# A transformer layer with AdaLN, window attention and an expert FFN: the input stage joined to attention

## The chip, the core and the metric

The kernel runs on one core of a Trainium2 chip. The core has five engines that run their own instruction streams and meet at semaphores: TensorE (PE; PEld is its weight load) multiplies, VectorE (DVE) and ScalarE (ACT) do elementwise work and reductions, GpSimd (POOL) does elementwise work more slowly and issues indirect transfers, and SyncE (SP) issues the other transfers, which 16 DMA engines carry out. The metric is the device time of one execution in microseconds (us).

## What is computed

The input has 2 batches of 2048 tokens with 256 values each. Per batch, six modulation rows come from a small vector c; two of them (ga, gb) are gates.

```
mod = (silu(c) @ wmod).reshape(B, 6, 1, -1)          # c: 2x256, wmod: 256x1536
sa, ca, ga, sb, cb, gb = the six rows of mod
ga, gb = (2 * (g >= 0) - 1) * maximum(abs(g), 0.25)  # each of them
h = layernorm(x) * (1 + ca) + sa
x = x + ga * attention(h, Wqkv, Wout)                # 16 heads of 64, causal window of 128
h = layernorm(x) * (1 + cb) + sb
x = x + gb * moe_ffn(h)                              # 8 experts, the 2 best for each token, capacity 640
```

## The kernel before

The 4096 tokens are 8 chunks of 512 (NC = 8), a chunk is 4 tiles of 128 (TILES), and 8 pairs of heads (PAIRS) stand for the 16 heads. All products with the weights are done with a value split in two fp16 parts, a high one and a low one, and three matmuls for each (SPLIT_PRODUCTS). So every weight is split before its first use: the high part is the scaled weight in fp16, the low part the scaled weight less the high part.

There are three blocks, each with one program for each engine, and a barrier of all engines between them. The first is the input stage, the second attention with routing, the third the FFN.

**Input stage.** SyncE issues, in this order: c (cT), all of the modulation weights (wmod, 1.5 MB, in the memory of k), the gate weights (gwT, gbB), the first chunk of x, Wqkv in three parts of 1 MB and Wout (stage 0 to 3; the first two lie where q will be, the others where attn will be), the other 28 tiles of x in one, and b1T. GpSimd makes the constants, then the rstd of chunk 0, then the low parts of stage 2 and 3. ScalarE waits for all the small loads, makes exp(-c), and then the high parts; stage 2 and 3 take it two passes. VectorE makes silu(c) and a copy of it spread over 128 columns (silB), the statistics and normalised rows xn of chunk 0, the modulation columns (modcol: ca and sa, with the features on the partitions), the low parts of stage 0 and 1, and the modulation rows. TensorE multiplies modcol's products and, with silB as weights, the rows' products on all 128 partitions, one batch after the other (score[0] and score[1]). VectorE makes modrow of them (the row of sb, 1 + cb and the two gates), again on all partitions and batch by batch.

**Attention's head.** VectorE clears the halos of k and v. TensorE transposes chunk 0's xn; ScalarE applies modcol to it (h32, ln_modulate); VectorE casts the high part (ln_high) and GpSimd subtracts the low part (ln_low). Then TensorE projects chunk 0 in pairs, q0, k0, q1, k1 and so on (HEAD_QK), through two PSUM banks (gen), which ScalarE empties. Then come the transposes of chunk 1's rows and LAG = 4 steps in which the scores of the first heads and the v projection of chunk 0 alternate. VectorE merges the scores, finds the maximum and normalises; ScalarE does the exponentials. For chunk 2 VectorE makes the statistics (ln_first(2)) and the normalised rows (ln_second(2)). From there chunk after chunk runs in one pattern: `scores`, `weighted_values`, `transposes`, and the projections of the next chunk between them.

**SyncE in attention.** It first fills slot_inputs in DRAM with empty rows (80 transfers), waits for them, and then stores the chunks. GpSimd waits for the same fill at the end of chunk 0, before the rstd for chunk 3. GpSimd's pieces in a chunk are the two masked copies for each unit (split_keys), the low part of the next rows, and, from chunk 1 on, the routing's scatter.

## Time and profile before

| | us |
|---|---|
| median of 3 runs | 1242.08 (1242.06 to 1242.58) |
| profiled execution | 1242.26 |
| its span, first to last instruction | 1240.5 |
| TensorE busy | 1131.4 (91%) |
| VectorE busy | 785.8 (63%) |
| ScalarE busy | 680.3 (55%) |
| GpSimd busy | 505.6 (41%) |

The busy shares are means over stages of different kinds. A window is a stretch of the span, with the busy time of each engine in it. In a row of the timeline the first number is the start and the second the length, both in us from the span's start, and a bracket at the end gives how long the engine had been idle before and what released it. A row can stand for several instructions (xN). L numbers are lines of the kernel before. "SPq" rows are issues of transfers: their length is the time that the issue took SyncE, and not that of the transfer.

### The profile page before, as it was taken

How to read it: one execution, taken by the hardware profiler on the slowest of the kernel's cores; microseconds unless marked ns; L12 is line 12 of the kernel's file. 1: busy time of each engine (PE TensorE's matmuls, PEld its weight loads, DVE VectorE, ACT ScalarE, POOL GpSimd, SP SyncE). 2: the span in 40 equal slices, each digit the busy share in tenths (PEclk: the TensorE clock that was granted, in tenths of full speed). 3: DMA queues.
4: the chain of work that ended last, by engine and by line, in shares of the span. 5: the costliest groups of instructions: out<-in, count | busy, mean ns of one | idle time of the engine just before them, and what ended most of it. 6: DMA issues, size and time to landing. Idle time of an engine off the chain costs nothing. (4 is left out here: it accounts for less than half of the span.)

```text
span 1240.5 us, 26348 instructions
## 1 busy us (share of the span) xinstructions
PE 1131.4 (91%) x10008; PEld 749.8 (60%) x10008; DVE 785.8 (63%) x1713; ACT 680.3 (55%) x1882; POOL 505.6 (41%) x558
## 2 busy tenths in 40 slices
PE   3799999999999999999999771499999999999996
PEld 2355565655655655656556551276868677686865
DVE  6366577486576575675865833476767667666754
ACT  4377657476477476475774721365472746547261
POOL 2134244454465255444544642414242434424242
PEclk9799999999999999999999975699999999999998
DMA  9641000100100001000002100613232233432000
GB/s 299 155 162 53 2 18 2 36 18 15 40 2 31 23 2 35 19 1 30 19 10 63 45 26 27 214 37 117 88 95 103 82 119 98 143 108 81 21 18 9
DMA packets 64858, 76.45 MB, mean 62 GB/s; under 512 B 18144, under 2 KB 56164, under 8 KB 64608
## 3 DMA queue, kind: packets, MB, share of 16 engines
q1 hardware_dynamic: 53984, 53.25, 13.5%
q0 software_dynamic: 10752, 21.54, 5.3%
q8 instruction: 80, 1.31, 0.5%
q14 instruction: 42, 0.34, 0.1%
HBM read 48.93 MB, written 33.78 MB: 67 GB/s over the span
## 5 line engine op out<-in xcount | busy, mean ns | idle before, releaser
L1230 ACT ACTIVATE hid<-up,b1T 128x512 f16<-128x512 f32 (+1 forms) x192 | 123.3, 642 | 196.1 <-PE up L1164 171.4
L1179 PE MATMUL down<-w,hid 128*128 128x256 f16 x1920 | 214.5, 273 | 0.0
L1164 PE MATMUL up<-xT,w 128*128 128x512 f16 (+1 forms) x1152 | 210.5, 344 | 0.0
L976 POOL TENSOR_SCALAR_AFFINE_SELECT probT_split<-probT 128x512 f32<-128x512 f32 x128 | 99.3, 776 | 261.7 <-ACT probT L688 261.1
L1179 PEld LDWEIGHTS down<-w,hid 128*128 128x128 f16 x1920 | 187.3, 98 | 23.1
L469 PE MATMUL gen<-hT,big 128*128 128x512 f16 x768 | 186.4, 382 | 10.9 <-ACT h2T L705 4.0
L680 ACT ACTIVATE prob<-score,negmax 128x128 f32<-128x128 f32 x512 | 180.4, 373 | 2.9 <-DVE negmax L797 2.9
L1120 POOL DMA_INDIRECT out<-y,rows x80 | 79.8, 998 | 238.3 <-DVE y L1296 226.0
L1164 PEld LDWEIGHTS up<-xT,w 128*128 128x128 f16 x1152 | 112.4, 98 | 93.3 <-issue 0.5
L1267 DVE TENSOR_TENSOR hid<-hid 128x512 f16<-128x512 f32 (+1 forms) x192 | 115.4, 607 | 77.1 <-ACT hid L1232 58.9
L792 DVE COPY_PREDICATED score<-above,score 128x512 f32<-128x512 int32 x128 | 88.4, 691 | 92.2 <-PE score L503 91.9
L688 ACT ACTIVATE probT<-pt 128x512 f32<-128x512 f32 x128 | 76.6, 598 | 106.2 <-PE pt L519 105.2
L1232 ACT ACTIVATE hid<-up,b1T 128x512 f32<-128x512 f32 (+1 forms) x192 | 123.6, 644 | 0.0
L469 PEld LDWEIGHTS gen<-hT,big 128*128 128x128 f16 x768 | 73.5, 98 | 80.6 <-ACT h2T L705 5.0
L503 PE MATMUL score<-k,q 64*64 64x192 f32 x2048 | 115.0, 339 | 0.2 <-ACT prob L680 0.2
L680 ACT ACTIVATION_READ_ACCUMULATOR prob<-score,negmax 128x1 f32 x512 | 109.7, 214 | 0.0
L1109 POOL DMA_INDIRECT kept<-out,rows x80 | 87.9, 1099 | 50.4 <-issue 30.2
L535 PE MATMUL pv<-probT_split,v 128*64 128x256 f32 x512 | 84.6, 409 | 18.8 <-POOL probT_split L978 12.2
L805 DVE TENSOR_TENSOR prob<-prob,rinv 128x512 f32<-128x512 f32 x128 | 100.1, 782 | 0.0
L503 PEld LDWEIGHTS score<-k,q 64*64 64x64 f32 x2048 | 64.8, 133 | 52.9 <-issue 49.5
L481 PE MATMUL gen<-big,hT 128*128 128x512 f16 x384 | 89.3, 379 | 0.0
L556 PE MATMUL gen<-wout,attn 128*128 128x256 f16 x768 | 87.8, 277 | 1.4 <-DVE attn L818 1.4
(133 smaller groups left out, 1582.5 us busy)
## 6 DMA issues: line engine op xcount, KB each, us to landing
big<-in_L_ffn_W SPq DMA_DIRECT2D x16, 1024.0 KB
slot_inputs<-empty_row SPq DMA_DIRECT2D x80, 129.5 KB, 2.4
rows<-slot_inputs SPq DMA_DIRECT2D x8, 1295.0 KB
out<-x SPq DMA_DIRECT2D x8, 512.0 KB, 3.3
x<-in_L_attn_x SPq DMA_DIRECT2D x1, 3584.0 KB, 23.5
q<-in_L_attn_Wqkv SPq DMA_DIRECT2D x2, 1024.0 KB, 7.7
k<-in_L_wmod SPq DMA_DIRECT2D x1, 1536.0 KB, 6.8
kept<-out,rows POOLq DMA_INDIRECT x80
```

The lines of the kernel that those rows point to most:

```text
L469: mm = pe.matmul(dst[:], wqkv[:, kd, a, col:col + P], hT[:, cn % 2, kd, b, :], start=(n == 0), stop=(n == 5))
L481: mm = pe.matmul(dst[:], hT[:, cn % 2, kd, a, s * P:(s + 1) * P], wqkv[:, kd, b, 2 * INNER + half * 512:2 * INNER + (half + 1) * 512], sta ...
L503: mm = pe.matmul(dst[lo:lo + HALF, 2 * hd + i, lo:lo + P + HALF], q[r:r + DH, j, b * P + lo:b * P + lo + HALF], k[r:r + DH, j, b * P + lo: ...
L680: mm = act.activation(prob[:, h % 2, b, :], score[h % 2][:, b, P:], ACT.Exp, bias=negmax[:, h % 2, b:b + 1], accum_out=rowsum[:, h % 2, b: ...
L792: dve.copy_predicated(sc[:, :, P:], above[:].bitcast(I32).unsqueeze(1).to_broadcast([P, TILES, P]), sc[:, :, 0:P])\
L805: dve.tensor_tensor(prob[:, h % 2], prob[:, h % 2], rinv[:, h % 2, :].unsqueeze(2).to_broadcast([P, TILES, P]), ALU.mult)\
L976: pool.affine_select(out=probT_split[:, h % 2, :, 1], in_=probT[:, h % 2], pattern=[[0, TILES], [1, P]], compare_op=ALU.is_ge, fill=zero, ...
L1164: mm = pe.matmul(bank[:, 0:size], w1[:, par, kd, a, ft * P:(ft + 1) * P], xT[:, par, b * KD + kd, lo:lo + size], start=(i == 0), stop=(i = ...
L1179: mm = pe.matmul(down[n][:, s, :], hid[:, ft, a, t * P:(t + 1) * P], w2[:, par, ft, b, :], start=(i == 0), stop=(i == 3 * FT - 1))
L1230: act.activation(hid[:, ft, 0, lo:lo + size], up[ft % 4][:, 0:size], ACT.Relu, scale=1 / W_SCALE, bias=bias).then_inc(hid_hi, 1)
L1232: act.activation(hid32[:, k_ % 4, 0:size], up[ft % 4][:, 0:size], ACT.Relu, scale=1 / W_SCALE, bias=bias).then_inc(up_out, 1)
L1267: dve.tensor_tensor(hid[:, ft, 1, lo:lo + size], hid32[:, k_ % 4, 0:size], hid[:, ft, 0, lo:lo + size], ALU.subtract).then_inc(hid_ready, 1)
```

## The change

- The first block is gone, and its work stands at the beginning of the attention block, each piece on its engine.
- SyncE issues the first chunk of x, then c, the columns' third of the modulation weights, the first two parts of Wqkv, the other two thirds of the modulation weights, the third part of Wqkv, the second chunk of x, Wout, the other 24 tiles, the gate weights. Then it waits for the modulation rows, stores them to DRAM, issues b1T and loads the rows back spread over all partitions (modrow). Only then comes the fill of slot_inputs.
- Weights are split in halves. ScalarE makes the high parts of stage 0 and 1, VectorE all low parts and both parts of stage 2 and 3; TensorE waits for the half that it needs (split_lo).
- Chunk 0 is projected q0 to q7, then k0 to k7. The rows' products, with silu(c) for both batches as 2 columns of weights, stand between k3 and k4, and their result lies on two partitions. VectorE makes the gates there (mod_gates).
- The halos are cleared on GpSimd, and VectorE subtracts the low part of chunk 0's rows.

```diff
-            HEAD_QK = sum([qk_pair(j) for j in range(PAIRS)], [])
+            HEAD_QK = [("q", j) for j in range(PAIRS)] + [("k", j) for j in range(PAIRS)]
...
+            def load_inputs(sp):
...
+                sp.dma_start(x[:, 0:TILES, :], xt[:, 0:TILES, :]).then_inc(x0_loaded, 16)
+                for b in range(B):
+                    sp.dma_start(cT[:, :, b], c_in[b].rearrange("(k p) -> p k", p=P), allow_slow_non_contiguous=True)\
+                      .then_inc(c_loaded, 16)
+                sp.dma_start(wmod[:, :, 0:2 * D], wm[:, :, 0:2 * D]).then_inc(mod_col_loaded, 16)
+                for i in range(2):
+                    sp.dma_start(stage_view[i], stage_src[i]).then_inc(stage_loaded[i], 16)
+                sp.dma_start(wmod[:, :, 2 * D:], wm[:, :, 2 * D:]).then_inc(mod_row_loaded, 16)
+                sp.dma_start(stage_view[2], stage_src[2]).then_inc(stage_loaded[2], 16)
+                sp.dma_start(x[:, TILES:2 * TILES, :], xt[:, TILES:2 * TILES, :]).then_inc(x1_loaded, 16)
+                sp.dma_start(stage_view[3], stage_src[3]).then_inc(stage_loaded[3], 16)
+                sp.dma_start(x[:, 2 * TILES:, :], xt[:, 2 * TILES:, :]).then_inc(x_loaded, 16)
...
+                sp.wait_ge(mod_row, 6)
+                sp.dma_start(mod_dram, mod_rows).then_inc(mod_stored, 16)
+                sp.dma_start(b1T[:].rearrange("p e f -> p (e f)"), b1_in.rearrange("e (f p) -> p (e f)", p=P),
+                             allow_slow_non_contiguous=True).then_inc(b1_loaded, 16)
+                sp.wait_ge(mod_stored, 16)
+                sp.dma_start(modrow[:], mod_dram.partition_broadcast(P)).then_inc(mod_spread, 16)
...
+            def weight_low(dve, i, h):
+                dve.wait_ge(split_hi, 2 * i + h + 1)
+                dve.scalar_tensor_tensor(stage_dst(i, h, 1), stage_half(i, h), W_SCALE, stage_dst(i, h, 0),
+                                         ALU.mult, ALU.subtract).then_inc(split_lo, 1)
+
+            def weight_both(dve, i, h):
+                dve.wait_ge(stage_loaded[i], 16)
+                dve.tensor_scalar(stage_dst(i, h, 0), stage_half(i, h), W_SCALE, None, ALU.mult).then_inc(split_hi, 1)
+                weight_low(dve, i, h)
...
+            def mod_row_products(pe):
+                pe.wait_ge(mod_row_loaded, 16)
+                silm = silT[:, 0, :].rearrange("p (k b) -> p k b", b=B)
+                for half in range(2):
+                    for kd in range(KD):
+                        mm = pe.matmul(mod_flat[:, half * 512:(half + 1) * 512], silm[:, kd, :],
+                                       wmod[:, kd, 2 * D + half * 512:2 * D + (half + 1) * 512],
+                                       start=(kd == 0), stop=(kd == KD - 1))
+                mm.then_inc(mod_mm, 1)
...
+                    load_inputs(sp)
+                    sp.wait_ge(rows_made, 2)
                     with sp.Fori(0, SLOTS // P) as i:
...
+                        if cn == 0 and j % 4 == 0:
+                            pe.wait_ge(split_lo, 1 + j // 4 + (2 if name[0] == "k" else 0))
...
+                    mod_col_products(pe)
                     ln_transposes(-1, 0, "ln0")
-                    for j in range(PAIRS):
-                        project_qk(-1, ("q", j))
-                        project_qk(-1, ("k", j))
+                    for name in HEAD_QK:
+                        if name == ("k", 4):
+                            mod_row_products(pe)
+                        project_qk(-1, name)
                     ln_transposes(-1, 1, "lnT")
+                    pe.wait_ge(mod_row, 6)
...
+                    small_constants(dve)
+                    silu(dve)
+                    dve.wait_ge(x0_loaded, 16)
+                    ln_first(0)
+                    ln_second(0)
+                    mod_columns(dve)
+                    weight_low(dve, 0, 0)
                     ln_high(-1, 0, "ln0")
-                    for n, name in enumerate(HEAD_QK):
-                        if n == 3:
-                            dve.wait_ge(x_loaded, 16)
-                            ln_first(1)
-                        if n == 5:
-                            ln_second(1)
+                    dve.wait_ge(ln_hi, 1)
+                    dve.tensor_tensor(hT[:, 0, :, 1, :], h32[:], hT[:, 0, :, 0, :], ALU.subtract).then_inc(ln_lo, 1)
+                    weight_low(dve, 0, 1)
+                    for h in range(2):
+                        weight_low(dve, 1, h)
+                    dve.wait_ge(x1_loaded, 16)
+                    ln_first(1)
+                    for h in range(2):
+                        weight_both(dve, 2, h)
+                    ln_second(1)
+                    mod_gates(dve)
                     ln_high(-1, 1, "lnT")
+                    for h in range(2):
+                        weight_both(dve, 3, h)
+                    gate_weights(dve)
+                    dve.wait_ge(x_loaded, 16)
                     ln_first(2)
```

On VectorE, between the cast of chunk 1's rows (hT<-h) and the first merge of scores (COPY_PREDICATED), this stands in a row before:

```order
58 L776 CAST hT<-h 128x2x512 [waits gen_free1,gen_free0]
59 L197 BN_STATS stats<-x 128x6 x4
60 L201 BN_AGGR meanvar<-stats 128x2 [waits ln_stat]
61 L201 BN_AGGR meanvar<-stats 128x2 x3
62 L792 COPY_PREDICATED score<-above,score 128x4x128 [waits scores_done]
```

and this now:

```order
44 L810 CAST hT<-h 128x2x512 [waits gen_free1,gen_free0]
45 L394 TENSOR_SCALAR wout<-attn 128x4x256 [waits stage_loaded3]
46 L389 SCALAR_TENSOR_TENSOR wout<-attn,wout 128x4x256 [waits split_hi]
47 L394 TENSOR_SCALAR wout<-attn 128x4x256 [waits stage_loaded3]
48 L389 SCALAR_TENSOR_TENSOR wout<-attn,wout 128x4x256 [waits split_hi]
49 L399 TENSOR_SCALAR gate<-gwT 128x2x8 [waits gate_loaded]
50 L401 SCALAR_TENSOR_TENSOR gate<-gwT,gate 128x2x8 [waits sil]
51 L209 BN_STATS stats<-x 128x6 [waits x_loaded]
52 L209 BN_STATS stats<-x 128x6 x3
53 L213 BN_AGGR meanvar<-stats 128x2 [waits ln_stat]
54 L213 BN_AGGR meanvar<-stats 128x2 x3
55 L826 COPY_PREDICATED score<-above,score 128x4x128 [waits scores_done]
```

The split of Wout (wout<-attn, from the staging memory) and of the gate weights has moved between the cast and the statistics.

On TensorE, where the row products stand in the changed program (L437; L486 are the projections, L471 the transposes of chunk 1's rows, L522 the scores):

```order
27 L486 MATMUL gen<-hT,big 128x512 [waits gen_free1]
28 L486 MATMUL gen<-hT,big 128x512 x5
29 L437 MATMUL score<-v,silT 2x512 [waits mod_row_loaded]
30 L437 MATMUL score<-v,silT 2x512 x3
31 L486 MATMUL gen<-hT,big 128x512 [waits gen_free0,split_lo]
32 L486 MATMUL gen<-hT,big 128x512 x5
```

Before, these products were 8 matmuls of 128x512 in the block ahead of the barrier; now 4 of 2x512 stand among the projections.

## Rows read from the trace of the kernel before

**Rows 1.** Windows: us, busy us (xinstructions) of five engines, clock, DMA, GB/s

```profile
0.00:35.40 35.40, 12.12 (x32) 7.04 (x33) 22.71 (x55) 12.84 (x8) 10.84 (x14) 0.90 0.98 282
75.00:149.00 74.00, 73.52 (x714) 42.19 (x713) 48.61 (x95) 53.49 (x189) 26.29 (x35) 1.00 0.18 63
```

**Rows 2.** Timeline of TensorE: start, length, line, operation, tiles [idle before <-releaser]

```profile
11.51 3.58 PE L332 MATMUL gen<-silT,k 128*128 128x2 f32 x16 [11.51 <-DVE silT L278]
14.94 8.68 PE L340 MATMUL score<-k,silB 128*128 128x512 f32 x16
35.41 1.94 PE L456 MATMUL gen<-identf,xn 128*128 128x128 f32 x8 [11.79 <-PEq L219]
41.23 22.95 PE L469 MATMUL gen<-hT,big 128*128 128x512 f16 x96 [3.87 <-POOL hT L967]
```

**Rows 3.** Timeline of SyncE's issues and of ScalarE's first activation

```profile
4.86 3.50 SPq L229 DMA_DIRECT2D gbB<-in_L_ffn_gate_b  x1
8.39 0.43 SPq L231 DMA_DIRECT2D x<-in_L_attn_x  x1
...
10.63 0.20 ACT L317 ACTIVATE silT<-cT 128x4 f32<-128x4 f32 x1 [8.54 <-DMA gbB<-in_L_ffn_gate_b]
...
17.26 10.95 SPq L235 DMA_DIRECT2D b1T<-in_L_ffn_b  x1
```

**Rows 4.** DMA view, 0 to 40 us: GB/s in 1-us slices; an issue, KB, us to landing

```profile
GB/s 0 0 45 98 369 393 430 243 5 21 194 379 381 401 401 406 430 414 430 372 361 350 346 347 348 351 345 348 349 351 345 347 322 61 10 7 14 114 169 217
...
x<-in_L_attn_x SPq DMA_DIRECT2D x1, 512.0 KB, 4.2
```

**Rows 5.** Timeline of VectorE and ScalarE, 12 to 20 us

```profile
12.57 1.41 DVE L197 BATCH_NORM_STATS2 stats<-x 128x6 f32<-128x256 f32 x4 [0.36 <-DMA x<-in_L_attn_x]
...
15.58 1.91 ACT L323 ACTIVATE big<-q 128x2048 f16<-128x2048 f32 x1 [4.74 <-DMA q<-in_L_attn_Wqkv]
15.88 1.38 DVE L207 TENSOR_SCALAR xn<-x,meanvar,rstd 128x256 f32<-128x256 f32 x4 [1.49 <-POOL rstd L215]
...
17.52 2.29 DVE L296 SCALAR_TENSOR_TENSOR big<-q,big 128x2048 f16<-128x2048 f32 x1
```

**Rows 6.** Timeline, 38 to 42 us: cast and low part of chunk 0's rows

```profile
38.28 0.69 DVE L776 CAST hT<-h 128x1024 f16<-128x1024 f32 x1 [0.63 <-ACT h L650]
...
39.05 2.12 POOL L967 TENSOR_TENSOR hT<-h,hT 128x1024 f16<-128x1024 f32 x1 [6.15 <-DVE hT L776]
```

**Rows 7.** Windows, columns as in rows 1 (the clock is third from the end)

```profile
20.00:23.60 3.60, 3.60 (x9) 1.33 (x7) 3.54 (x5) 2.89 (x3) 0.00 (x0) 1.00 1.10 353
45.00:46.00 1.00, 1.00 (x5) 0.45 (x4) 0.00 (x0) 0.00 (x0) 0.00 (x0) 0.79 0.43 150
```

**Rows 8.** Timeline of VectorE and TensorE, 66 to 74 us

```profile
66.45 0.69 DVE L776 CAST hT<-h 128x1024 f16<-128x1024 f32 x1 [22.54 <-ACT h L650]
...
68.78 0.68 DVE L792 COPY_PREDICATED score<-above,score 128x512 f32<-128x512 int32 x1
...
72.43 0.68 DVE L805 TENSOR_TENSOR prob<-prob,rinv 128x512 f32<-128x512 f32 x1
...
73.39 0.66 PE L519 MATMUL pt<-identf,prob 128*128 128x128 f32 x4
```

**Rows 9.** Timeline of VectorE and GpSimd, 24 to 29 us

```profile
24.63 4.07 POOL L253 TENSOR_TENSOR big<-attn,big 128x2048 f16<-128x2048 f32 x1 [8.79 <-ACT big L323]
...
25.88 3.11 DVE L310 SCALAR_TENSOR_TENSOR modrow<-gated 128x256 f32<-128x256 f32 x1
```

**Rows 10.** Timeline of TensorE late in attention

```profile
683.01 0.65 PE L535 MATMUL pv<-probT_split,v 128*64 128x256 f32 x4 [2.20 <-DVE attn L818]
```

**Rows 11.** Window of the same place, columns as in rows 1

```profile
682.00:688.00 6.00, 4.99 (x45) 3.22 (x45) 5.14 (x13) 3.19 (x17) 3.18 (x3) 0.72 0.69 242
```

**Rows 12.** Timeline: the fill of slot_inputs, and what GpSimd does behind its wait

```profile
35.60 66.91 SPq L434 DMA_DIRECT2D slot_inputs<-empty_row  x80
...
149.69 0.23 POOL L213 TENSOR_SCALAR rstd<-meanvar 128x4 f32<-128x4 f32 x1 [5.46 <-DVE meanvar L201]
```

More of the change, by code:

```diff
@@ new lines, in make_constants @@
+            def make_constants(pool):
+                pool.memset(onesf[:], 1.0)
+                pool.memset(identf[:], 0.0).then_inc(consts, 1)
+                pool.wait_ge(consts, 1)
+                pool.affine_select(out=identf[:], in_=identf[:], pattern=[[-1, P]], compare_op=ALU.not_equal,
+                                   fill=1.0, base=0, channel_multiplier=1)
+                pool.affine_select(out=above[:], in_=onesf[:], pattern=[[1, P]], compare_op=ALU.is_gt,
+                                   fill=0.0, base=0, channel_multiplier=-1)
+                pool.iota(token_no[:], pattern=[[P, NT]], base=0, channel_multiplier=1, allow_small_or_imprecise_dtypes=True)
+                pool.iota(expert_no[:], pattern=[[1, E]], base=0, channel_multiplier=0,
+                          allow_small_or_imprecise_dtypes=True).then_inc(consts, 1)
+                pool.memset(k[:, :, 0:P], 0.0).then_inc(k_halo, PAIRS)
+                pool.memset(v[:, 0, :], 0.0).then_inc(v_halo, 2)
+                reciprocal_std(pool, meanvar[0], rstd[0], ln_mv, ln_var, ln_rstd, 1)
@@ L1015, in _ @@
                     zero = pool.to_reg(0.0)
-                    ln_low(0)
+                    make_constants(pool)
                     ln_rstd_of(1)
```

231 lines of the change are left out of this document (103 added, 128 removed).

## The prediction

> **What bounds the kernel now.** I read the busy time by stage first. From 75 us TensorE is busy for 73.52 of 74 us, while in the first 35.4 us it is busy for 12.12 [rows 1]. Everything behind the start of attention therefore runs at TensorE's pace, and the change does not touch it; what can move is the moment at which TensorE gets there. The timeline of TensorE shows how it does [rows 2]: small products from 11.51, the products for the modulation rows from 14.94 to 23.62, nothing until the barrier between the two blocks, transposes at 35.41, the first projection at 41.23, and from there one unbroken run to 64.18. The question is how much earlier than 41.23 the first projection can start, what new work stands in TensorE's line behind it, and whether the softmax of the first heads follows as fast.
>
> **The start.** The order in which loads are issued is the first term. ScalarE's exponential, which opens the chain to the modulation columns, runs at 10.63 although its own input is issued first of all; it waits for every small load, and the last of those, gbB, was issued only at 4.86 and held the queue until 8.36 [rows 3]. The first tokens were issued behind it, at 8.39, and landed 4.2 us later [rows 3, 4]. Bandwidth was nearly nil in the microseconds around 8 and then some 380 to 430 GB/s [rows 4]. In the changed order the tokens are issued at 0.8 (the barrier that all engines pass at the program's start is unchanged): 0.8 + 4.2 = 5.0. The two loads of c follow at once; I take 5.2. The first third of the modulation weights (0.5 MB) adds 0.52 MB / 400 GB/s = 1.3 us: 6.3. Wqkv's first part (1.05 MB) adds 2.6: 9.2 with some slack, the second 11.8, the other two thirds of the modulation weights 14.4, the third part 17, the second tokens 18.3, Wout 21, the rest of x (3.1 MB at 350 GB/s) 30.
>
> VectorE: the exponential at 5.2, silu done at about 6.05 (in the trace the column products start 0.88 after the exponential: 10.63 to 11.51, [rows 2, 3]). Then statistics from 6.05 and normalised rows. From the start of the statistics to the end of xn the trace takes 17.26 - 12.57 = 4.69 [rows 5], so xn is there at 10.8. TensorE's column products take 3.58 [rows 2] from 6.3 to 9.9 and are covered. Transposes start at 10.85. ScalarE has split the two halves of the first weights by then (1.91 for both [rows 5], 9.2 to 11.2). From the start of the transposes to the end of the cast hT<-h the trace takes 38.97 - 35.41 = 3.56 [rows 2, 6]. The low part, 2.12 on GpSimd [rows 6], goes to VectorE, where a two-input operation over 128x2048 takes 2.29 [rows 5], so 1.15 to 1.2 for half of it. The first projection starts at 10.85 + 3.56 + 1.25 = 15.7 instead of 41.23: **25.5 us earlier**. VectorE's split of the first half of q's weights (1.15) fits between 11.2 and the cast. The splits behind it end at 16.9, 18.1 and 19.3; q0's copy needs the second of these at 18.3 and q4's the fourth at 24, so none is waited for.
>
> Bounds on this term: if Wqkv's first part lands 3 us later, ScalarE comes to the modulated rows that much later less 0.8, so the first projection starts at 18; if c comes with the tokens, at 15.0.
>
> **Row products in TensorE's line.** They now stand between k3 and k4. Before, 8 matmuls, 16 records of 512 columns, took 8.68 us [rows 2], 0.54 each with the slow ones at the beginning; from 20 us on 9 are begun in 3.60 us [rows 7], 0.40 each. With both batches in one pass there are 4 matmuls, 8 records: 3.2 to 4.3 us, and by 0.43 for a record **3.45 us on the path**, which were free before. The first projections run at the low clock, half of the high one: from 45 to 46 us it is 0.79 on average, so it rises in that microsecond [rows 7], nearly 4 us behind the first projection, and the 22.95 us of the run hold that [rows 2]; I keep the cost, since TensorE comes to the projections after a pause now as well. So k7 ends, and the first scores come, 25.5 - 3.45 = **22.0 us earlier**, at 43.4. The gates' six VectorE instructions start when the row products end, at 36.4; none reads more than 512 elements of each of two partitions, so each is below the 0.68 of a 128x512 operation [rows 8]: done by 40.5. TensorE waits for them before the scores, at 43.4, and does not feel it; without that cover they would cost up to 4.
>
> **What VectorE now owes at the worst place.** Between the cast for the second chunk's rows and the first softmax step VectorE used to have only ln_first(2): cast at 66.45, merge at 68.78 [rows 8]. The changed order puts the whole split of wout there (two times one scaled copy and one two-input subtraction over 128x1024) and the gate weights. The subtraction is 1.15 to 1.2 as above. The scaled copy is as the cast of the same size, 0.69 [rows 6]; upper bound 1.2, if it runs as slowly as the subtraction. The gate weights are two tiny operations, 0.35 to 0.4. Sum 2 x (0.69 + 1.2) + 0.4 = 4.2, at most 5.2.
>
> To this I add a block. VectorE's last operation of a gate row took 3.11 us, from 25.88 to 28.99, for 256 elements, an eighth of what takes 2.29 in rows 5; GpSimd's two-input subtraction ran from 24.63 to 28.70 [rows 9]. A VectorE operation with two inputs in SBUF waited until GpSimd was through. Now GpSimd's ln_low(1) (2.12 us) starts 0.08 after the cast, just as it did, but beside it VectorE no longer has the statistics, whose 1.64 us from the cast's end to the merge show no stretching [rows 8], but wout's split. The scaled copy runs, the subtraction behind it then waits until GpSimd ends: cast end + 0.1 + 2.12 instead of + 0.7, which is 1.5 more. So the first merge comes 4.2 + 1.5 = 5.7 later than it would by a pure shift. TensorE, after the two pairs of v groups, waits for the first exponentials; in the trace it ran on into the third scores and began the first head's transpose at 73.39, with 0.3 us to spare over the normalised rows (72.43 + 0.68 = 73.11) [rows 8]. **TensorE stands still for 5.4 us**; bounds 3.9 (no block) and 7.
>
> The Trainium skill (SBUF — State Buffer, Who interferes with whom) goes further: a scaled copy inside SBUF can itself take the pair of ports that VectorE and GpSimd share, and whoever comes first keeps it for the whole instruction. By that, GpSimd would start 0.6 later and the sum would have 6.0 instead of 5.4 and end at 1227.5. No row shows the case.
>
> **The clock behind that pause.** Late in attention TensorE stood 2.20 us until 683.01 [rows 10], and over the 6 us around that the granted clock is 0.72 on average [rows 11], a mixture of the two levels (2.4 and 1.2 GHz); 6 x 0.28 = 1.7 us of full work were lost. After 5.4 us of standing I expect the same again, less the little that hides in the gap between the third scores and the transpose: **1.4 us**; bounds 0 and 2.2.
>
> **Sum.** 25.5 - 3.45 - 5.4 - 1.4 = 15.2 us earlier at the end of the first scores' phase. From there TensorE is the bound [rows 1] and the shift stays. The profiled execution is 1242.26 us (span 1240.5 and 1.8 around it), the median 1242.08: 1242.1 - 15.2 = **1226.9**.
>
> **Behind it.** SyncE now issues the rows' store, b1T and the spread load before the fill of slot_inputs. The store waits for the gates, 40; b1T's issue took 10.95 and the fill 66.91 [rows 3, 12]. So 40 + 0.5 + 11 + 0.5 + 67 = 119. GpSimd waits for the fill before its rstd of 149.69 [rows 12], now at 134.5: 15 us of slack. The spread rows are read at the end of chunk 0, also past 130, and landed long before. Halos on GpSimd, one barrier less, the silB copy gone: nobody waits for these.
>
> **Rivals.**
> (a) VectorE and GpSimd do not block each other there and the clock holds: 25.5 - 3.45 - 3.9 = 18.2, **1223.9**. For it: the scaled copy may let GpSimd in late or share; against it: [rows 9 to 11].
> (b) The loads are not as early: c or the first weights land 2 to 3 us later, because many small packets stand ahead. The rest follows: 15.2 - 2.5 = 12.7, **1229.4**. For it: bandwidth needed two microseconds to rise after the first issues [rows 4].
> (c) The clock is up before or early in the first projections, since TensorE has worked on the column products and transposes shortly before: up to 2 us more, **1225**.
> (d) Slower than before: the fill. It starts only behind b1T. Each us by which it ends after 134.5 holds GpSimd, then the normalised rows of chunk 3, then TensorE. The kernel is slower than before only when it ends after 149.7, 31 us later than in my sum, that is if each of its 80 issues takes 1.2 instead of 0.84 us: **1243 and more**. Against it: nothing else stands on the queue by then, and 0.84 us each (66.91 / 80) is what they take beside the same attention work.
> (e) The change does not do what it says: the loads gain nothing, and attention is tied to them. In the trace the first weights reach ScalarE at 15.58 [rows 5]. With the same moment in the new kernel, ScalarE splits until 17.5, and the modulated rows, cast and low part take it to 21.2 (1.63 for the rows' share of the 3.56, 0.8, 1.25): 5.5 later than in the main case, **1232.4**, still faster than before, since the barrier and the modulation rows that VectorE made before it are gone from the path.
>
> **How the numbers follow.** Main case 0.55; (a) 0.17; (b) 0.15; (c) 0.08; (d) 0.02; (e) 0.03. The main case with its bounds spans 1224.5 to 1229.5; (a), (b) and (c) lie within 1222 to 1232, and (e) and (d) are what I leave out. What a measurement of this kernel can tell from no change is about 0.2%, 2.5 us; all cases but (d) are beyond it, and (d) may end inside it: faster 0.97, same 0.01, slower 0.02.
>
> **What would show it.** The first 128x512 projection at 15 to 18 us; the 2-row products 3.4 us long near 33; the first scores near 43.4; the gates done before them. Then the wout split on VectorE, a subtraction stretched to well over 2 us beside GpSimd's ln_low, and TensorE idle for 5 us before the third scores, with a granted clock of 0.5 behind it. From 75 us on each event 15 us earlier than before. I am wrong if the first projection starts after 19, if TensorE waits for weights within q and k, or if the shift seen at 70 us is not that of the last instruction.

## The result, and the profile after

The changed kernel takes **1229.88 us** (median of 4 runs, 1227.74 to 1230.35); the kernel before, measured beside it, 1242.07 (4 runs, 1241.98 to 1242.58). The ratio is 0.9901, interval 0.9888 to 0.9913: 12.2 us less, where 15.2 were predicted. The profiled execution was the fastest of the four, 1227.74 us with a span of 1226.0. The same pair in two later jobs is 14.4 and 11.8 us apart (below), so the gain itself is known to within 1 to 2 us.

TensorE's timeline of the changed kernel, which answers to [rows 2] and [rows 8]. Columns: start, length, engine, line, operation, output and inputs, count; in brackets how long the engine had been idle and what released it.

```profile
7.05 3.54 PE L428 MATMUL pt<-silT,v 128*128 128x2 f32 x16 [7.05 <-DMA v<-in_L_wmod]
15.52 17.20 PE L486 MATMUL gen<-hT,big 128*128 128x512 f16 x72 [2.93 <-DVE hT L974]
32.65 3.59 PE L437 MATMUL score<-v,silT 128*2 128x512 f32 x8
42.80 0.56 PE L522 MATMUL score<-k,q 64*64 64x192 f32 x8
...
47.18 2.76 PE L500 MATMUL gen<-big,hT 128*128 128x512 f16 x12
55.19 0.92 PE L522 MATMUL score<-k,q 64*64 64x192 f32 x8 [5.24 <-ACT prob L708]
```

The first projection (L486) starts at 15.52, was 41.23; the row products (L437) stand in the line with 3.59 us; the first scores (L522) start at 42.80, were 65.45. Then TensorE stands for 5.24 us.

VectorE's timeline over the same place, and GpSimd's row beside it; it answers to [rows 8] and [rows 9].

```profile
36.28 0.41 DVE L409 COPY h<-score 2x256 f32<-2x256 f32 x1 [10.60 <-PE score L437]
...
38.97 0.68 DVE L416 SCALAR_TENSOR_TENSOR h<-gated,prob 2x512 f32<-2x512 f32 x1
43.80 0.70 DVE L810 CAST hT<-h 128x1024 f16<-128x1024 f32 x1 [4.15 <-ACT h L676]
44.41 0.69 DVE L394 TENSOR_SCALAR wout<-attn 128x1024 f16<-128x1024 f32 x1
45.13 3.03 DVE L389 SCALAR_TENSOR_TENSOR wout<-attn,wout 128x1024 f16<-128x1024 f32 x1
48.08 0.68 DVE L394 TENSOR_SCALAR wout<-attn 128x1024 f16<-128x1024 f32 x1
48.80 1.23 DVE L389 SCALAR_TENSOR_TENSOR wout<-attn,wout 128x1024 f16<-128x1024 f32 x1
...
52.08 0.70 DVE L826 COPY_PREDICATED score<-above,score 128x512 f32<-128x512 int32 x1
```

```profile
44.57 2.51 POOL L1017 TENSOR_TENSOR hT<-h,hT 128x1024 f16<-128x1024 f32 x1 [21.14 <-DVE hT L810]
```

The two subtractions L389 are the same operation on the two halves of wout. The one that began beside GpSimd's took 3.03 us, the other 1.23. From the cast to the first merge (L826) it is 8.28 us; before it was 2.33 [rows 8]. VectorE had stood idle for 10.60 us before the gates (L409) and for 4.15 before the cast.

Windows of the changed kernel (start and end, length, busy time of PE, PEld, DVE, ACT and POOL with counts, granted clock, DMA share, GB/s), which answer to [rows 1] and [rows 11]. The last is from the first scores to the output projection of chunk 0.

```profile
54.00:56.00 2.00, 0.81 (x15) 0.71 (x17) 1.03 (x4) 2.00 (x9) 0.00 (x0) 0.50 1.01 221
58.00:60.00 2.00, 2.00 (x7) 0.78 (x6) 1.79 (x4) 0.53 (x1) 1.40 (x2) 0.62 0.83 227
60.00:62.00 2.00, 2.00 (x23) 0.91 (x20) 0.00 (x0) 1.21 (x3) 0.28 (x1) 1.00 0.56 164
42.80:136.89 94.09, 88.37 (x817) 49.43 (x817) 62.57 (x124) 61.13 (x213) 32.47 (x42) 0.96 0.45 126
```

Behind the stop the clock is at the lower of its two levels, 1.2 GHz (0.50), and it rises again shortly before 60: 0.62 on average from 58 to 60, 1.00 behind it. The number behind each busy time counts every instruction that runs in the window, also one that began before it.

SyncE's issues (length: what the issue took SyncE) and GpSimd's rstd of chunk 3, which answer to [rows 3] and [rows 12].

```profile
15.36 13.52 SPq L329 DMA_DIRECT2D gwT<-in_L_ffn_gate_w  x2
...
39.67 0.32 SPq L333 DMA_DIRECT2D mod_rows<-h  x1
40.04 0.39 SPq L334 DMA_DIRECT2D b1T<-in_L_ffn_b  x1
...
45.49 66.17 SPq L449 DMA_DIRECT2D slot_inputs<-empty_row  x80
```

```profile
134.40 0.23 POOL L225 TENSOR_SCALAR rstd<-meanvar 128x4 f32<-128x4 f32 x1 [5.46 <-DVE meanvar L213]
```

The fill is issued by 111.7, 22.7 us ahead of the rstd, which is released by VectorE's statistics and not by the fill.

To see where 15 became 12, I set four moments of TensorE side by side, in us from each span's start: first projection, first scores, output projection of chunk 0, and the first down product of the first expert in the third block. "Again" and "side" are the changed kernel in two more jobs (below).

| | before | after | again | side |
|---|---|---|---|---|
| first projection | 41.23 | 15.52 | 15.72 | 15.54 |
| first scores | 65.45 | 42.80 | 44.15 | 43.72 |
| output projection, chunk 0 | 152.18 | 136.89 | 138.81 | 138.27 |
| first down product | 817.04 | 802.42 | 803.32 | 804.52 |
| span | 1240.5 | 1226.0 | 1226.8 | 1228.0 |
| shift to before: at chunk 0 / at the end | | 15.3 / 14.5 | 13.4 / 13.7 | 13.9 / 12.5 |

### The profile page after: what moved, and what is told of

It reads as the page before. It is cut to its first block and busy times, and to the rows that moved or that the text cites. A ratio compares the mean times of both kernels' runs of the same rounds, so it can differ in the third digit from the quotient of the medians.

```text
span 1226.0 us, 26328 instructions
## 1 busy us (share of the span) xinstructions
PE 1127.6 (92%) x10000; PEld 747.3 (61%) x10000; DVE 788.0 (64%) x1709; ACT 672.4 (55%) x1880; POOL 500.9 (41%) x557
## 5 line engine op out<-in xcount | busy, mean ns | idle before, releaser
L486 PE MATMUL gen<-hT,big 128*128 128x512 f16 x768 | 186.0, 381 | 10.0 <-ACT h2T L733 4.0
L826 DVE COPY_PREDICATED score<-above,score 128x512 f32<-128x512 int32 x128 | 88.5, 691 | 91.7 <-PE score L522 91.4
L486 PEld LDWEIGHTS gen<-hT,big 128*128 128x128 f16 x768 | 73.4, 98 | 79.7 <-ACT h2T L733 5.0
L522 PE MATMUL score<-k,q 64*64 64x192 f32 x2048 | 115.1, 339 | 5.4 <-ACT prob L708 5.4
L522 PEld LDWEIGHTS score<-k,q 64*64 64x64 f32 x2048 | 64.9, 133 | 57.9 <-issue 55.0
```

The lines of the kernel that those rows point to most:

```text
L486: mm = pe.matmul(dst[:], wqkv[:, kd, a, col:col + P], hT[:, cn % 2, kd, b, :], start=(n == 0), stop=(n == 5))
L522: mm = pe.matmul(dst[lo:lo + HALF, 2 * hd + i, lo:lo + P + HALF], q[r:r + DH, j, b * P + lo:b * P + lo + HALF], k[r:r + DH, j, b * P + lo: ...
```

## Experiments

All kernels compute the whole result. Unless another is named, each is the changed kernel with one edit. Three jobs ran on three chips, with the kernel before at 1242.27, 1241.47 and 1241.76 us (7, 13 and 9 runs); ratios are to the one of the same job.

### What stands between the cast and the first softmax

The theory: TensorE's stop comes from VectorE's 8.28 us, 1.8 of which (3.03 - 1.23) are the block by GpSimd, and the low clock comes from the stop.

> The changed kernel once more, with a profile of its own. Its four times lie at 1227.74 and at 1229.58 to 1230.35, and the profile that I have is of the fastest; TensorE's run up to the end of attention is fixed by waits that are in the program. Theory: the 2.4 us between the executions lie behind attention, in the stretch where TensorE's granted clock falls and rises again (last routing and first expert), as 1.4 us of the first expert do between the profiles of before and after. Then this profile, if its time is near 1230, has the first output projection at 136.9 us as before, and the difference behind 640 us. Rival: it lies in the start (loads, clock of the first projections); then the first output projection comes at 138 to 139.5 us.

Measured: 1227.84 us (1227.51 to 1228.55), ratio 0.9883 [0.9866, 0.9899]. The stop is 5.23 us in this execution too. The expectation's rival came true: the output projection of chunk 0 comes at 138.81, 1.9 later than in the first profile, and 1.35 of that stand ahead of the first scores. Behind chunk 0 this execution is 1.0 shorter, so both parts vary.

**The statistics first** (`stats_first`). The same work, only that what runs beside GpSimd has one input.

```diff
                     ln_high(-1, 1, "lnT")
+                    dve.wait_ge(x_loaded, 16)
+                    ln_first(2)
                     for h in range(2):
                         weight_both(dve, 3, h)
                     gate_weights(dve)
-                    dve.wait_ge(x_loaded, 16)
-                    ln_first(2)
```

> Behind the cast of chunk 1's rows VectorE makes chunk 2's statistics first and wout's split and the gate weights after them; the work is the same. Theory of the block (a two-input VectorE operation waits for GpSimd's two-input one): the first subtraction of the split, 3.03 us beside GpSimd's low part, falls to 1.2 to 2.3 (GpSimd's short rstd may still catch it), so the first merge comes at 50.3 to 51.3 us instead of 52.08 and the kernel is 0.8 to 1.8 us faster than the changed one, 1228.1 to 1229.1. Rival (the 3.03 us are the operation's own, or come from the transfers beside it): the subtraction stays at 3 us and the time at 1229.9.

Measured: 1227.30 us (1226.9 to 1228.31), 0.9881 [0.9865, 0.9898]. VectorE's and GpSimd's timelines:

```profile
45.23 0.69 DVE L810 CAST hT<-h 128x1024 f16<-128x1024 f32 x1 [4.15 <-ACT h L676]
45.84 1.40 DVE L209 BATCH_NORM_STATS2 stats<-x 128x6 f32<-128x256 f32 x4
...
47.56 1.12 DVE L394 TENSOR_SCALAR wout<-attn 128x1024 f16<-128x1024 f32 x1
48.72 1.23 DVE L389 SCALAR_TENSOR_TENSOR wout<-attn,wout 128x1024 f16<-128x1024 f32 x1
...
52.11 0.70 DVE L826 COPY_PREDICATED score<-above,score 128x512 f32<-128x512 int32 x1
```

```profile
46.00 2.13 POOL L1017 TENSOR_TENSOR hT<-h,hT 128x1024 f16<-128x1024 f32 x1 [22.41 <-DVE hT L810]
48.10 0.67 POOL L225 TENSOR_SCALAR rstd<-meanvar 128x4 f32<-128x4 f32 x1
48.85 1.99 POOL L227 TENSOR_TENSOR rstd<-rstd,half_neg 128x4 f32<-128x4 f32 x1
```

Both subtractions now take 1.23 us and GpSimd's 2.13 instead of 2.51: that block is gone, and it was the meeting with GpSimd that made it. Cast to merge is 6.88 instead of 8.28, and TensorE's stop 3.84 instead of 5.23. So moving the statistics took away 1.4 us of the stop. The other 3.8 are nearly all plain work: the first scaled copy still takes 1.12 instead of 0.69, since GpSimd's subtraction runs until 48.13. The median fell by 0.5, less than the stop did; the two kernels' ranges overlap, so the time alone shows nothing here, the trace does. (The merge stands at 52.11, as in the changed kernel, because the first scores came 1.4 us later in this execution, at 44.23.)

This run also answers a rival of the prediction, that without the block the clock holds. It does not: behind the wait of 3.84 us the granted clock is 0.50.

```profile
56.00:58.00 2.00, 2.00 (x14) 1.12 (x9) 2.00 (x6) 1.72 (x10) 0.00 (x0) 0.50 0.99 195
```

**Wout's split ahead of the gates** (`wout_early`): into the 10.60 us in which VectorE stood idle.

```diff
                     ln_second(1)
-                    mod_gates(dve)
-                    ln_high(-1, 1, "lnT")
                     for h in range(2):
                         weight_both(dve, 3, h)
+                    mod_gates(dve)
+                    ln_high(-1, 1, "lnT")
                     gate_weights(dve)
```

> Only wout's split moves ahead of the gates on VectorE, into the 10.6 us in which it waits for the row products. Theory: the first merge comes 5.7 us earlier, at 46.4; TensorE's waits of 5.24 and 0.5 us before the third scores and the first transpose fall to 0.1, and with them the low clock behind the wait, worth 1.4 us. Together 7 us less than the changed kernel: 1222.9, between 1222 and 1224.5. Rival (the low clock there comes whatever the wait): 5.6 us less, 1224.3, with a granted clock under 0.9 between 46 and 52. Rival (something else holds the third scores, such as v's copies): under 4 us.

Measured: 1223.93 us (1223.43 to 1225.38), 0.9856 [0.984, 0.9873]: 3.9 less than the unchanged copy beside it. VectorE, and TensorE behind it:

```profile
45.57 0.17 DVE L399 TENSOR_SCALAR gate<-gwT 128x16 f16<-128x16 f32 x1
45.78 2.12 DVE L401 SCALAR_TENSOR_TENSOR gate<-gwT,gate 128x16 f16<-128x16 f32 x1
47.81 1.39 DVE L209 BATCH_NORM_STATS2 stats<-x 128x6 f32<-128x256 f32 x4
```

```profile
52.76 0.56 PE L522 MATMUL score<-k,q 64*64 64x192 f32 x8 [1.64 <-ACT prob L708]
...
54.05 0.66 PE L538 MATMUL pt<-identf,prob 128*128 128x128 f32 x4 [0.36 <-DVE prob L839]
```

The time lies in the expected range, but the first merge comes at 49.65 and not at 46.4, and the stop did not go away: 1.64 + 0.36 = 2.0 us stay. A subtraction of 16 elements a partition, which takes 0.18 in `stats_first`, takes 2.12, the length of GpSimd's subtraction that began 0.04 before it. The clock held, though (full level from the first scores to chunk 0), and the scores of 0.92 us above take 0.56.

**All of it ahead** (`all_early`): wout's split, the statistics of chunk 2 and the gate weights, in that order, and then the gates and the cast.

```diff
                     ln_second(1)
-                    mod_gates(dve)
-                    ln_high(-1, 1, "lnT")
                     for h in range(2):
                         weight_both(dve, 3, h)
-                    gate_weights(dve)
                     dve.wait_ge(x_loaded, 16)
                     ln_first(2)
+                    gate_weights(dve)
+                    mod_gates(dve)
+                    ln_high(-1, 1, "lnT")
```

> Wout's split, the gate weights and chunk 2's statistics all stand ahead of the gates, so that the first merge follows the cast. Theory: TensorE was at its own pace in this place in the kernel before, with 0.3 us to spare, so this gives 0 to 0.3 us more than moving wout's split alone: 1222.5. Rival (VectorE's softmax still sets the pace of the first steps): the 2.2 us by which the first merge moves come through, 1220.7.

Measured: **1220.29 us** (1218.99 to 1221.7), 0.9826 [0.981, 0.9843]: 7.55 less than the unchanged copy, 3.6 less than `wout_early`. The rival of the expectation held: what still stood between cast and merge was not free. Windows from the first scores to chunk 0's output projection, of `again` and of `all_early`:

```profile
44.15:138.81 94.66, 88.95 (x818) 49.57 (x818) 62.54 (x124) 61.13 (x213) 32.47 (x42) 0.96 0.44 125
```

```profile
44.19:130.93 86.74, 86.26 (x818) 48.44 (x818) 55.50 (x110) 61.20 (x213) 32.14 (x42) 1.00 0.48 136
```

Of the 7.92 us between them TensorE is busy for 2.69 (the low clock) and idle for 5.23 (the stop). The second stretch is as long as that of the kernel before, 86.73. So the stop and its clock cost 7.4 to 7.9 us in all, and the late place of VectorE's work was their whole cause: nothing was left out, and both are gone.

The same stretch, from the first scores to chunk 0's output projection, in all of these executions (us; idle is the length less TensorE's busy time):

| | length | TensorE busy | idle |
|---|---|---|---|
| before | 86.73 | 86.25 | 0.48 |
| changed kernel: first profile | 94.09 | 88.37 | 5.72 |
| changed kernel: `again` | 94.66 | 88.95 | 5.71 |
| `stats_first` | 92.26 | 87.94 | 4.32 |
| `wout_early` | 88.86 | 86.38 | 2.48 |
| `all_early` | 86.74 | 86.26 | 0.48 |

Here the steps are cleaner than in the medians, which the rest of the program blurs. Moving wout's split brought 5.2 to 5.8 us in this place, where the median shows 3.9, and the rest of the move 2.1, where the medians are 3.6 apart.

### Where the gain of the change comes from

**The old order of loads** (`old_loads`): c, the modulation weights, the gate weights, then the tokens and Wqkv, in the joined kernel.

```diff
-                sp.dma_start(x[:, 0:TILES, :], xt[:, 0:TILES, :]).then_inc(x0_loaded, 16)
                 for b in range(B):
                     sp.dma_start(cT[:, :, b], c_in[b].rearrange("(k p) -> p k", p=P), allow_slow_non_contiguous=True)\
                       .then_inc(c_loaded, 16)
...
                 sp.dma_start(wmod[:, :, 2 * D:], wm[:, :, 2 * D:]).then_inc(mod_row_loaded, 16)
...
                 sp.dma_start(gbB[:], gate_b.partition_broadcast(P)).then_inc(gate_loaded, 16)
+                sp.dma_start(x[:, 0:TILES, :], xt[:, 0:TILES, :]).then_inc(x0_loaded, 16)
+                for i in range(4):
+                    sp.dma_start(stage_view[i], stage_src[i]).then_inc(stage_loaded[i], 16)
```

> The changed kernel with the loads in the order of the kernel before (c, modulation weights, gate weights, first chunk of x, Wqkv, Wout, the rest). Theory (the first term of my sum: the order sets when chunk 0's tokens are there, 12.6 us as in the kernel before, since the gate weights' issues hold the queue until 8.4): xn ends at 17.3, the first projection starts at 22.1 instead of 15.5 to 15.7, and the kernel is 6.5 us slower than the changed one: 1234.4 where that has 1227.8 to 1229.9. Rival (the joining of the blocks brings nearly all of it, and the order little): under 2 us slower.

Measured: 1235.32 us (1233.47 to 1235.9), 0.9944 [0.9928, 0.9961].

```profile
17.68 1.97 PE L469 MATMUL gen<-identf,xn 128*128 128x128 f32 x8 [7.72 <-DVE xn L219]
22.59 17.65 PE L484 MATMUL gen<-hT,big 128*128 128x512 f16 x72 [2.93 <-DVE hT L972]
```

The first projection starts at 22.59, 6.9 to 7.1 later than in the three executions with the new order, and still 18.6 before that of the kernel before. The transposes wait for the normalised rows, and these for the tokens. The kernel is 6.2 us faster than the one before: in the place behind the first scores it loses as much as the changed kernel does (94.30 us for the stretch of the table).

**The new order alone** (`loads_alone`): the kernel before with its barrier; x, c, the modulation weights and all Wqkv and Wout are issued ahead of the gate weights, whose split stands behind the modulation rows.

```diff
+                    sp.dma_start(x[:, 0:TILES, :], xt[:, 0:TILES, :]).then_inc(x0_loaded, 16)
...
-                    sp.dma_start(wmod, wmod_in.rearrange("(k p) n -> p k n", p=P)).then_inc(small_loaded, 16)
...
+                    sp.dma_start(wmod, wmod_in.rearrange("(k p) n -> p k n", p=P)).then_inc(mod_loaded, 16)
                     for i in range(4):
                         sp.dma_start(stage_view[i], stage_src[i]).then_inc(stage_loaded[i], 16)
...
+                    dve.wait_ge(gate_loaded, 16 * (KD + 1))
+                    dve.tensor_scalar(gate16[:, :, 0, :], gwT[:], W_SCALE, None, ALU.mult).then_inc(sil, 1)
```

> The kernel before, with its barrier and everything else, but with the new kind of order: first chunk of x, c, modulation weights, Wqkv, Wout, then the gate weights and the rest of x; the gate weights are split at the end of VectorE's stage. Theory: the input stage is a chain of loads, ScalarE's splits, GpSimd's low parts and VectorE's rows that starts 4 to 5 us earlier and ends at 30.5 instead of 34.9; first projection at 36.5 to 37, time 1237.7. Rival (the rest of x, issued later, comes too late for the second chunk's statistics): 1240 to 1243, with VectorE's statistics of chunk 1 waiting for the load.

Measured: 1239.92 us (1238.05 to 1241.93, 10 runs), 0.9989 [0.9979, 0.9998]: 1.5 us less, where 1237.7 was expected. The ranges of the two kernels overlap (the one before: 1239.42 to 1244.08), but the interval of the ratio leaves 1 out. TensorE's two rows, then VectorE's and GpSimd's in the input stage:

```profile
32.69 1.94 PE L458 MATMUL gen<-identf,xn 128*128 128x128 f32 x8 [10.18 <-PEq L220]
38.51 23.84 PE L471 MATMUL gen<-hT,big 128*128 128x512 f16 x96 [3.87 <-POOL hT L969]
```

```profile
22.98 3.08 DVE L307 SCALAR_TENSOR_TENSOR modrow<-gated 128x256 f32<-128x256 f32 x1
28.01 2.25 DVE L307 SCALAR_TENSOR_TENSOR modrow<-gated 128x256 f32<-128x256 f32 x1
```

```profile
21.71 4.07 POOL L254 TENSOR_TENSOR big<-attn,big 128x2048 f16<-128x2048 f32 x1 [12.16 <-ACT big L325]
25.74 4.24 POOL L254 TENSOR_TENSOR wout<-attn,wout 128x2048 f16<-128x2048 f32 x1
```

The tokens and weights come earlier, but the barrier waits for VectorE's modulation rows, and behind the row products (13.62, were 14.94) these keep their pace: two of their operations still take 3.08 and 2.25 us beside GpSimd's low parts, as that of [rows 9] did, and TensorE stands for 10.18 us. Of the 25.7 us at the first projection such an order alone brings 2.7; within the joined kernel the changed order brings 7, and the joining without it 18.6 (`old_loads`). The 96 projections then take 23.84 us, 0.9 more than before, so 1.8 of the 2.7 are left at the first scores.

**The row products last** (`rows_last`): `all_early` with the row products behind k7.

```diff
                     for name in HEAD_QK:
-                        if name == ("k", 4):
-                            mod_row_products(pe)
                         project_qk(-1, name)
+                    mod_row_products(pe)
```

> all_early with the row products behind k7 instead of behind k3, so that the gates no longer lie beside four projections. The prediction held that this cover hides up to 4 us. The transposes of chunk 1's rows (1.7 us) still cover a part: gates end 3.4 us after the products, scores start 2.2 to 2.4 us later than in all_early: 1222.6 against 1220.3. Rival (the cover is worth nothing since TensorE has slack there): 1220.3.

Measured: 1223.99 us (1222.16 to 1225.46), 0.9862 [0.9846, 0.9879].

```profile
46.45 0.56 PE L522 MATMUL score<-k,q 64*64 64x192 f32 x8 [2.43 <-DVE h L416]
```

Without k4 to k7 as cover TensorE waits 2.43 us for the gates. The prediction gave up to 4 for it; the transposes of chunk 1, which need no gate, cover the rest. The medians of `rows_last` and `all_early` are 3.7 us apart, but they come from two jobs, and the runs of `rows_last` alone spread over 3.3; the first scores come 2.3 us later.

### The clock, and the spread behind attention

**TensorE kept busy ahead of the projections** (`warm`): `all_early` with matmuls added whose result nobody reads.

```diff
+            def keep_busy(pe, n):
+                for _ in range(n):
+                    pe.matmul(pv[:, 0:P], identf[:], identf[:], start=True, stop=True)
...
+                    pe.wait_ge(consts, 2)
+                    keep_busy(pe, 9)
                     mod_col_products(pe)
                     ln_transposes(-1, 0, "ln0")
+                    keep_busy(pe, 10)
```

> all_early with 19 matmuls of 128x128 on the identity that nobody reads: 9 before the column products, 10 behind the transposes of chunk 0's rows, where TensorE otherwise waits for the cast and the low part. Theory (the low clock of the first projections costs 2.0 to 3.0 us: 72 projections take 17.1 to 18.5 us instead of 72 x 0.2145 = 15.45): with the clock up they take 15.5, the transposes ahead 1.1 instead of 1.97, and the kernel is 2.5 to 3.7 us faster than all_early: 1217. Rival (a): the extra matmuls delay the column products or the first projection by as much as they bring: 1220.3 or more. Rival (b): the clock does not come up by them: the same.

Measured: 1218.15 us (1216.36 to 1220.54), 0.9818 [0.9801, 0.9834].

```profile
12.46 3.69 PE L434 MATMUL pv<-identf 128*128 128x128 f32 x20
15.99 15.70 PE L490 MATMUL gen<-hT,big 128*128 128x512 f16 x72
```

The 72 projections ahead of the row products take 15.70 us here, 17.20 in the profiled execution of the changed kernel and 18.34 in `again`. So the low clock at the start costs the changed kernel 1.5 to 2.6 us, and another amount in each execution. The first scores come at 41.78, 2.4 us ahead of those of `all_early`; the medians of the two jobs are 2.1 apart, a little less than expected.

The last job compares on one chip: the changed kernel (`after_side`), `all_early` (`early_side`), `warm` (`warm_side`), and `warm` with 44 more such matmuls at the third block's beginning (`warm_both`).

```diff
+                    for _ in range(44):
+                        pe.matmul(up[3][:, 0:P], ident16[:], ident16[:], start=True, stop=True)
                     row_transposes(0, 0, range(DG))
```

> The changed kernel again, beside its three variants on one chip. In two jobs its medians were 1229.9 and 1227.8; I expect 1227.5 to 1230, and the output projection of chunk 0 between 136.9 and 138.8 us.

> all_early again. Theory: 7.4 us less than the changed kernel on the same chip (5.24 + 0.54 of waits and 1.5 of low clock), with a spread of 2 to 3 us left. Rival: the 7.5 us of the first job were partly the chip's or the clock's luck; then under 6.

> warm again: 72 first projections at the full clock from the start, 15.7 us instead of 17.1 to 18.5. Theory: 2.4 us less than all_early on the same chip. Rival: less than 1, since what is saved at the start is lost where the clock falls late in attention.

> warm, with 44 more matmuls of 128x128 on the identity ahead of the row transposes of the third block, where TensorE waits 6 us for the rows. In the profiles so far the first 96 products of the first expert took 20.72 or 20.88 us in some and 22.0 to 22.3 in others, with the granted clock at 0.5 when they or the transposes begin. Theory: they take 20.72 in every run and the transposes ahead are shorter; 1 to 2.5 us less than warm on the same chip, and a spread under 2 us. Rival: VectorE's copies of the transposes set that place; then 0 to 1 us less.

| | median us (range, runs) | ratio to before | chunk 0's output projection to first down |
|---|---|---|---|
| after_side | 1229.94 (1229.73 to 1230.46, 4) | 0.9909 [0.9893, 0.9924] | 666.25 |
| early_side | 1221.08 (1219.4 to 1221.98, 5) | 0.9833 [0.982, 0.9847] | 666.26 |
| warm_side | 1219.56 (1216.29 to 1221.97, 5) | 0.982 [0.9804, 0.9837] | 666.30 |
| warm_both | 1219.0 (1218.16 to 1220.87, 5) | 0.9824 [0.9811, 0.9838] | 665.40 |

`all_early` is 8.9 us faster than the changed kernel, their runs far apart. Of the 8.7 between the two spans, 7.8 stand between the first scores and chunk 0 (94.55 and 86.72 us for the stretch of the table above); the other 0.9 is the low clock at the start, which was shorter in this execution, and no merit of the move. `warm`'s 1.5 more and `warm_both`'s 0.6 lie within the spread. In the two profiled executions `warm` is 1.6 us ahead at the first scores and 1.5 at the end; the times do not settle that it is worth this in every execution, nor that the 44 matmuls are worth anything.

What makes the spread: that last column is 664.86 in the kernel before, 665.53 and 664.51 in the first two executions of the changed kernel, and 662.99 (`all_early`) and 662.63 (`warm`) where the same programs took 666.26 and 666.30 above. From the output projection of chunk 0 to that of chunk 6, the last but one, all agree within 0.1 us (512.3). Windows from chunk 6's output projection to the first down product, `warm` and then `warm_side`, the same program:

```profile
640.80:791.10 150.30, 91.34 (x879) 63.01 (x878) 78.23 (x187) 60.46 (x170) 55.47 (x62) 0.81 0.22 73
```

```profile
640.30:794.30 154.00, 94.89 (x879) 64.83 (x878) 78.19 (x187) 60.63 (x170) 55.95 (x62) 0.78 0.22 72
```

879 records in both, 3.55 us more busy time at the lower mean clock, and 3.7 us more length. Some of it stands in the first expert's up products, here of `after_side` and of `again`:

```profile
782.50:804.50 22.00, 22.00 (x99) 9.76 (x97) 12.26 (x18) 19.17 (x31) 7.35 (x8) 0.94 0.49 157
```

```profile
782.60:803.30 20.70, 20.70 (x99) 9.41 (x97) 11.22 (x16) 17.55 (x29) 7.38 (x8) 1.00 0.52 171
```

`warm_both` has the short form of these (20.72), but so had `again` without the added matmuls, so one execution doesn't show that they secured it. Why the clock falls for longer in one execution of a program than in another, no run here shows.

## Why the prediction was right, and where it was off

The direction, the mechanism and the range held: 1229.88 lies within 1222 to 1232, 3.0 above 1226.9. How near it came is partly chance: the gain was 12.2, 14.4 and 11.8 us in the three jobs that have the changed kernel, where 15.2 were predicted, so it was too high in each. Step by step:

- **The start, 25.5 us.** Right: the exponential at 5.15 (5.2 in the working), the first projection at 15.52 to 15.72 (15.7). That loads late by 2 to 3 us (rival b) or loads that gain nothing (e) did not happen; `old_loads` shows that the order alone would have cost 7 of it.
- **Row products in TensorE's line, 3.45.** 3.59. (The x9 of [rows 7] is not nine begun in 3.60 us: one was running at 20.00, eight begin, 0.43 us apart. The sum used 0.43.) The gates are done at 39.65 (40.5), 3 us before the first scores; `rows_last` shows what the cover was worth, 2.4.
- **The clock of the first projections.** The step "I keep the cost" was too simple. From first projection to first scores, less 3.53 for the row products, it is 23.75 us in the profiled execution, 24.65 in `after_side` and 24.90 in `again`, 24.22 before. The first scores came 22.65, 21.73 and 21.30 us earlier, not 22.0. The level rises at 18.56, 21.07 and 20.41 us in `after`, `again` and `after_side`, which is 3.0, 5.4 and 4.9 us behind the first projection, and 4.2 behind it in the kernel before. Rival (c), a clock that is up early, is `warm`'s 15.70, and it took added matmuls.
- **The wait, 5.4.** 5.24, from 8.28 - 2.33 = 5.95 more on VectorE (5.7 in the working) less what TensorE had to spare. The block was there: 3.03 - 1.23 = 1.8 on the subtraction, and `stats_first` took 1.4 off TensorE's stop.
- **The clock behind it, 1.4.** This is the term of the sum that was mis-sized: TensorE was busy for 88.37 and 88.95 us over the stretch instead of 86.26, so 2.1 to 2.7. It was read off a pause of 2.20 us; behind 5.24 the low level lasted from before 54 to past 58. Rival (a), no block and a clock that holds, did not happen. With the block gone and 3.84 us of waiting (`stats_first`; 3.9 in the rival) the clock still fell and TensorE was busy for 1.7 us more; it held only in `wout_early`, behind waits of 1.64 and 0.36.
- **"From there the shift stays."** This step failed, by up to 1.4 us (the prediction itself named a shift that changes on the way as a sign of being wrong). From chunk 0 to chunk 6 it stays to 0.1. From there to the first expert the same program varies by 3.7 us, together with TensorE's clock. [rows 10] and [rows 11] lie in that stretch; the prediction took a price from them and did not count the place itself as one that varies.
- **The fill (rival d).** 22.7 us of slack. b1T's issue took 0.39 and not 11, with only the rows' store in front of it. The spread load behind it then took 4.09 where the sum had 0.5; together the fill began at 45.49 instead of 52.

For the execution next to the median (`after_side`, 1229.77) the miss sums up: 0.3 at the first scores, 1.0 behind them (7.8 against 6.8), 1.4 behind chunk 0; 15.2 - 2.7 = 12.5, the difference of the spans. For the first profiled one the first scores were 0.65 better, the stretch behind them 0.55 worse (7.35), and 0.8 was lost later: 14.5.

The Trainium skill (SBUF — State Buffer, Who interferes with whom) says that a scaled copy within SBUF can take the port pair that VectorE and GpSimd share, and that whoever comes first keeps it for the whole instruction. The traces agree, both ways round. In the changed kernel GpSimd's subtraction began 0.16 behind wout's scaled copy and took 2.51 instead of 2.12. In `stats_first` the scaled copy began at 47.56, while GpSimd's subtraction ran until 48.13, and took 1.12 instead of 0.69; GpSimd's first rstd operation (0.67, otherwise 0.23) began at 48.10 and ended 0.1 behind that copy. The price by that rule was put at 0.6 us. On VectorE it was 0.4 (2.51 - 2.12), and it is part of the 8.28; what it was worth on TensorE no run separates, since the whole wait was 5.24, below both 5.4 and 6.0.

## What to carry to other kernels

When a barrier is removed, look at what the joined engine now owes between the last operand of a phase and its first result, and move all of it that has its data into the idle stretch in front: here that was worth 7.4 to 7.9 us by the traces, beside the 12.2 of the change itself, and 5.2 to 5.8 with the largest piece alone moved. An operation with two inputs in SBUF is priced by what GpSimd runs beside it, and not by its size alone. A wait on the bounding engine can cost the clock behind it on top of its own length (1.7 us behind 3.84, 2.1 to 2.7 behind 5.24, nothing behind 1.64 and 0.36), so wait and busy time are to be compared separately over the same stretch. And where executions of one program differ by several us, a step of 1 or 2 us is read between two moments of the trace, not from the medians.

## What was not expected of the hardware

- A two-input subtraction over 128x16 took 2.12 us beside GpSimd, 0.17 otherwise. With wout's split moved away, the block simply fell on the next operation with two inputs.
- SyncE's issue of the two small gwT transfers took 13.52 us with more than 3 MB queued in front, and that of b1T 0.39 with 8 KB in front where it had taken 10.95 behind 3.5 MB. The duration of an issue depends on what stands in front of it, so it can't be carried to another place.
- The column of the granted clock doesn't show the low clock at the start of the changed kernel. These are windows of the changed kernel and of the kernel before:

```profile
16.50:17.50 1.00, 1.00 (x4) 0.30 (x3) 1.00 (x2) 0.00 (x0) 0.00 (x0) 1.00 1.06 354
```

```profile
43.20:44.20 1.00, 1.00 (x4) 0.32 (x3) 0.70 (x3) 0.20 (x1) 0.00 (x0) 0.50 0.41 141
46.20:47.20 1.00, 1.00 (x7) 0.41 (x5) 0.00 (x0) 0.48 (x1) 0.00 (x0) 1.00 0.52 177
```

  At the lower level 4 projections run in a microsecond's window, at the upper 7, counting those that began before it. In the changed kernel the column says 1.00 while 4 run. The trace's first record of the clock in this execution is its rise to the full level, at 18.56 us; before it there is none, and the view then prints 1.00. The starts of the projections agree: they are 0.43 us apart up to 18.48 and 0.22 from 18.74 on. `warm`'s first record is a rise at 15.17, ahead of its first projection.
- The same program differs by 3.7 us between chunk 6's output projection and the first expert, more than half of what moving wout's split brought.
